# Cross-attention with layer norm: scores from two 64-row halves of the TensorE array

## The chip, the cores and the metric

One core of one Trainium2 chip. The metric is the device time of one execution in microseconds. Five engines work side by side and meet at semaphores: TensorE (PE in the profile; its weight loads, PEld, are listed apart), VectorE (DVE), ScalarE (ACT), GpSimd (POOL) and SyncE (SP), which issues the DMA transfers.

## The reference

Batch 4, 2048 queries and 77 context rows each, width 512, 16 heads of 32. Everything is float32.

```python
qs  = (q @ wq).reshape(Bq, Lq, H, HD).transpose(0, 2, 1, 3)
ks_ = (k @ wk).reshape(Bq, Lk, H, HD).transpose(0, 2, 1, 3)
vs  = (v @ wv).reshape(Bq, Lk, H, HD).transpose(0, 2, 1, 3)
scores = einsum('bhqd,bhkd->bhqk', qs, ks_) / sqrt(HD)
scores = where(mask[:, None, :, :], -inf, scores)
attn_w = softmax(scores, axis=-1)
attn = einsum('bhqk,bhkd->bhqd', attn_w, vs)
out = attn.transpose(0, 2, 1, 3).reshape(Bq, Lq, H * HD) @ wo + q
out = (out - mean) / sqrt(var + EPS) * gamma + beta
```

q is x; k and v are both the context.

## The kernel before

The 8192 query rows are 64 tiles of 128. Everything of a tile is done in two halves of eight heads. To keep float32 accuracy with float32r matmuls, each operand is kept as a high part and a low part (qh and ql, kh and kl, and so on), and each product is three matmuls: high by high, high by low, low by high.

TensorE's order is written out in the loop over t behind L336. For a tile it is: scores of half 0; the output projection of an earlier tile (project_o, 12 matmuls of 512 columns); the transposes of the previous tile's probabilities, half 0 (transpose_p, five of 128 x 128); scores of half 1; the query projection for the tile four ahead (project_q, 12 matmuls of 512 columns); the transposes of half 1. Once in four tiles (t in FIRST, 4, 8, ...) weigh_v follows the scores of half 1, and once (t in SECOND, 5, 9, ...) it follows the scores of half 0. weigh_v multiplies the transposed probabilities of four tiles by the values, in pieces of the array of 64 rows by 32 columns (L315): the keys 0 to 63 from vm, the last 13 from vr.

**Scores.** The heads of a tile come in four groups of four. Partition 32 j + d of qh[:, g] is dimension d of head j of group g, 128 rows in all. kh[:, g, b] is block-diagonal, 4 x 77 = 308 columns: head j's keys stand in rows 32 j to 32 j + 31 and in columns 77 j to 77 j + 76, the rest is zero (memsets L485 and L612; the blocks are filled by L429 and L491). So three matmuls of 308 columns with the query as weights give a bank of scores for 128 queries and four heads, and a half tile is two banks, six matmuls, one after the other (L283). p_s counts one up after each bank.

**Their reader.** VectorE waits for a bank's p_s, adds the mask and writes to pr (L520), twice, then takes the negated maximum of the eight heads (L526). ACT exponentiates head by head (L406, eight instructions), VectorE sums (L533) and inverts (L535), POOL scales into pn (L632, L634), TensorE transposes pn (L293, L295), and ACT copies the result to ptr (L375), which weigh_v reads. VectorE and ACT carry out their instructions in written order, the work for the norm and for the query splits among them. A score block may overwrite a bank once VectorE has read it (v_st).

Of the kernel before, what the change touches and what calls it, by code (L numbers as in the profile page):

```python
# [5 lines left out]
P = 128  # L6
NB, LQ, D, H, HD, LK = 4, 2048, 512, 16, 32, 77
# [3 lines left out]
TB = LQ // P  # L11
GW = 4 * LK
NG = 4
# [23 lines left out]
def outputs(t):  # L37
    return OUTPUTS.get(t, ())


def cross_attention_layernorm(nc, x, xT, ctxT, mask, wq, wk, wv, wo, gamma, beta, out):
    f32, f32r, u8 = mybir.dt.float32, mybir.dt.float32r, mybir.dt.uint8
    ALU = mybir.AluOpType
# [10 lines left out]
    with ctx:  # L54
        def sb(name, shape, dt=f32):
            return ctx.enter_context(nc.sbuf_tensor(name, shape, dt))

        def sem(name):
            return ctx.enter_context(nc.semaphore(name))
# [2 lines left out]
        wql = sb("wql", [P, KT, D], f32r)  # L62
        woh = sb("woh", [P, KT, D], f32r)
        wol = sb("wol", [P, KT, D], f32r)
        kh = sb("kh", [P, NG, NB, GW], f32r)
        kl = sb("kl", [P, NG, NB, GW], f32r)
        vm = sb("vm", [P, NB, 2, 4, HD])
        vr = sb("vr", [P, NB, 2, 4, HD])
        msk = sb("msk", [P, 2, TB, LK], u8)
# [24 lines left out]
        with ExitStack() as start:  # L94
            def early(name, shape):
# [16 lines left out]
        SB, PTB, AVB, MB = bank[0:2], bank[2:4], bank[4:6], bank[6:8]  # L112
# [10 lines left out]
        p_k, p_v, p_q, p_s, p_tp, p_pv, p_o = (  # L123
            sem(n) for n in ("p_k", "p_v", "p_q", "p_s", "p_tp", "p_pv", "p_o"))
# [4 lines left out]
        v_z, v_w, v_k, v_pf, v_ps, v_ql, v_st, v_max, v_sum, v_rec, v_al, v_res, v_bs, v_bn, v_y = (  # L129
            sem(n) for n in ("v_z", "v_w", "v_k", "v_pf", "v_ps", "v_ql", "v_st", "v_max", "v_sum", "v_rec",  # L130
                             "v_al", "v_res", "v_bs", "v_bn", "v_y"))
# [104 lines left out]
        def _(pe):  # L236
            for k in range(KT):
                pe.wait_ge(d_k[k], 32)
                for g in range(NG):
                    mm = nc.tensor.matmul(bank[g][:, 0:NB * LK], wk_sb[:, k, g * P:(g + 1) * P], ctx_sb[:, k, :],  # L240
                                          start=(k == 0), stop=(k == KT - 1))
# [3 lines left out]
            def project_v(b):  # L245
                if b == 0:
                    pe.wait_ge(d_wv, 16)
                if b >= 2:
                    pe.wait_ge(a_v, b - 1)
                for k in range(KT):  # L250
                    last = nc.tensor.matmul(AVB[b % 2][0:LK, :], ctx_sb[:, k, b * LK:(b + 1) * LK], wv_sb[:, k, :],
                                            start=(k == 0), stop=(k == KT - 1))
                last.then_inc(p_v, 1)
# [15 lines left out]
                        n += 1  # L269
                last.then_inc(p_q, 1)  # L270

            def scores(t, groups):
                blk, r = t // 4, t % 4
                for g in groups:
                    i = NG * t + g
                    if t == 0:
                        pe.wait_ge(v_k, 4 * g + 4)
                    pe.wait_ge(v_ql, 4 * blk + g + 1)
                    if i >= 2:
                        pe.wait_ge(v_st, i - 1)  # L280
                    o = SB[i % 2][:, 0:GW]
                    for n, (w, s) in enumerate(((qh, kh), (qh, kl), (ql, kh))):
                        last = nc.tensor.matmul(o, w[blk % 2][:, g, r * P:(r + 1) * P], s[:, g, t // TB, :],  # L283
                                                start=(n == 0), stop=(n == 2))
                    last.then_inc(p_s, 1)

            def transpose_p(t, half):
                n = 2 * t + half
                pe.wait_ge(g_norm, n + 1)
                if n >= 1:  # L290
                    pe.wait_ge(a_pt, n)
                for s in range(4):
                    last = nc.tensor.transpose(PTB[0][:, s * P:(s + 1) * P], pn[:, half, s, :], ident[:])  # L293
                last.then_inc(p_tp, 1)
                nc.tensor.transpose(PTB[1][:, 0:P], pn[:, half, 4, :], ident[:]).then_inc(p_tp, 1)  # L295

            def weigh_v(e):
                t, n, half = STEPS[e]
                b, cols = t // TB, columns(e)
                if e == 0:  # L300
                    pe.wait_ge(d_vm[0], 160)
                    pe.wait_ge(d_vm[1], 160)
                pe.wait_ge(a_pt, 2 * (t + n - 1) + half + 1)
                if e == 0:
                    pe.wait_ge(a_v, NB)
                elif e < E - 1:
                    pe.wait_ge(v_al, 2 * e)
                else:
                    pe.wait_ge(v_st, NG * T)
                for v, first in ((vm, True), (vr, False)):  # L310
                    for j in range(4):
                        for gi in range(2):
                            rows = slice(KM * gi, KM * gi + KM)
                            c = j if first else 4
                            mm = nc.tensor.matmul(av_bank(e, gi)[HD * j:HD * (j + 1), 0:n * P], v[rows, b, half, j, :],  # L315
                                                  ptr[rows, half, c, cols], start=first, stop=not first)
                            if not first and j == 3:
                                mm.then_inc(p_pv, 1)

            def project_o(t):  # L320
                r = t % 4
                misc_free(pe, ("o", t))
                o = misc_bank(("o", t))
                n = 0
                for k in range(KT):
                    pe.wait_ge(v_al, 2 * STEP_OF[t, k // 2] + k % 2 + 1)
                    for w, s in ((ah, woh), (ah, wol), (al, woh)):
                        last = nc.tensor.matmul(o[:], w[:, k, r * P:(r + 1) * P], s[:, k, :],  # L328
                                                start=(n == 0), stop=(n == 3 * KT - 1))
                        n += 1  # L330
                last.then_inc(p_o, 1)
# [1 line left out]
            for i in range(4):  # L333
                project_q(i)
            for t in range(T):
                scores(t, (0, 1))  # L336
                if t == 0:
                    project_v(0)
                if t == 1:
                    pe.wait_ge(g_id, 2)  # L340
                if t in SECOND:
                    weigh_v(SECOND[t])
                elif outputs(t):
                    project_o(outputs(t)[0])
                if t >= 1:
                    transpose_p(t - 1, 0)
                scores(t, (2, 3))
                if t < 3:
                    project_v(t + 1)
                if t in SECOND:  # L350
                    if t == 5:
                        pe.wait_ge(a_w, KT + 1)
                        pe.wait_ge(v_w, KT + 1)
                    project_o(outputs(t)[0])
                for o in outputs(t)[1:]:
                    project_o(o)
                if t in FIRST:
                    weigh_v(FIRST[t])
                    transpose_p(t - 1, 1)
                if t + 4 < T:  # L360
                    project_q(t + 4)
                if t >= 1 and t not in FIRST:
                    transpose_p(t - 1, 1)
# [9 lines left out]
        def _(act):  # L373
# [51 lines left out]
            def keep_k(g):  # L425
                act.wait_ge(p_k, g + 1)
                for j in range(4):
                    rows = slice(32 * j, 32 * j + 32)
                    nc.scalar.activation(kh[rows, g, :, j * LK:(j + 1) * LK],  # L429
                                         bank[g][rows, 0:NB * LK].rearrange("p (b k) -> p b k", b=NB), ACT.Copy,  # L430
                                         scale=SCALE).then_inc(a_k, 1)

# [4 lines left out]
            for k in range(KT):  # L437
                act.wait_ge(d_wq[k], 16)
                keep(wqh[:, k, :], wq_raw[:, k, :]).then_inc(a_w, 1)
                keep_x(k)  # L440
            act.wait_ge(v_z, 1)
            keep_k(0)
            keep_k(1)
            keep_q(0)
            keep_k(2)
            keep_q(1)
            keep_k(3)
# [36 lines left out]
        def _(dve):  # L484
            nc.vector.memset(kh[:].bitcast(f32), 0.0).then_inc(v_z, 1)  # L485

            def low_k(g):
                for j in range(4):
                    rows = slice(32 * j, 32 * j + 32)
                    dve.wait_ge(a_k, 4 * g + j + 1)  # L490
                    nc.vector.scalar_tensor_tensor(  # L491
                        out=kl[rows, g, :, j * LK:(j + 1) * LK],
                        in0=bank[g][rows, 0:NB * LK].rearrange("p (b k) -> p b k", b=NB), scalar=SCALE,
                        in1=kh[rows, g, :, j * LK:(j + 1) * LK].bitcast(f32), op0=ALU.mult,
                        op1=ALU.subtract).then_inc(v_k, 1)

            def mask_all(b):
# [69 lines left out]
            for k in range(KT):  # L567
                dve.wait_ge(a_w, k + 1)
                nc.vector.tensor_tensor(wql[:, k, :], wq_raw[:, k, :], wqh[:, k, :].bitcast(f32),
                                        ALU.subtract).then_inc(v_w, 1)  # L570
            dve.wait_ge(g_z, 1)
            low_k(0)
            low_k(1)
            low_q(0)
            low_k(2)
            low_q(1)
            low_k(3)
# [128 lines left out]
```

## Time and profile before

| | |
|---|---|
| median of three runs | 698.63 us (698.15, 702.37, 698.63) |
| the profiled execution | 700.0 us, span 698.0 us |
| busy, share of the span | PE 92%, PEld 71%, DVE 76%, ACT 73%, POOL 70% |
| granted clock of TensorE over the span | 0.972 |

Busy time is the time in which at least one instruction of the engine is under way. A matmul's duration includes the time its result takes through the array, so matmuls that follow each other overlap in it: the distance between two starts tells what one takes of the engine. In a timeline a row holds one instruction, or a run of like ones with their count. In square brackets stands the idle time before a row and what ended it. Only PEld rows tell when weights begin to load.

### The profile page before, as it was taken

The numbers are of one execution on the slowest core, as the hardware profiler recorded it, in microseconds if no ns is written. First come the engines' busy times: TensorE is split into PE (matmuls) and PEld (weight loads), VectorE is DVE, ScalarE is ACT, GpSimd is POOL, SyncE is SP. The second block draws the span as 40 slices with busy tenths as digits, with TensorE's granted clock in tenths as the row PEclk, the third lists the DMA queues.
The fourth block names the chain that finished last, engine by engine and source line by source line (L and its number), as shares of the span: only waits on it lengthen the run. The fifth ranks groups of instructions, "written<-read, shape, count | busy, mean of one in ns | idle before, by whom it ended". The sixth has DMA issues, their size and how long they took to land. (4 is left out here: it accounts for less than half of the span.)

```text
span 698.0 us, 13011 instructions
## 1 busy us (share of the span) xinstructions
PE 640.0 (92%) x4096; PEld 497.2 (71%) x4096; DVE 529.6 (76%) x1006; ACT 511.5 (73%) x1562; POOL 490.3 (70%) x641
## 2 busy tenths in 40 slices
PE   7989799999999999999999999999999999987454
PEld 4657487777868686877778686868777786865333
DVE  5667587878888878877889878788779888785444
ACT  4667688778877887887787788878788787774340
POOL 6234457897877777788977787777888786775551
PEclk9989999999999999999999999999999999999776
DMA  8532112222231222212222222222222211112112
GB/s 274 190 96 43 32 61 71 83 91 76 92 101 63 88 78 92 89 64 91 91 87 91 65 88 77 92 92 69 83 92 77 77 61 46 62 46 61 61 45 76
DMA packets 36563, 57.78 MB, mean 83 GB/s; under 512 B 8592, under 2 KB 9616, under 8 KB 36496
## 3 DMA queue, kind: packets, MB, share of 16 engines
q1 hardware_dynamic: 36496, 56.96, 24.7%
q8 instruction: 34, 0.56, 0.3%
q14 instruction: 33, 0.27, 0.1%
HBM read 39.53 MB, written 16.78 MB: 81 GB/s over the span
## 5 line engine op out<-in xcount | busy, mean ns | idle before, releaser
L406 ACT ACTIVATE pr<-pr,nm 128x77 f32<-128x77 f32 x1024 | 269.9, 351 | 53.1 <-DVE nm L526 52.9
L632 POOL TENSOR_TENSOR pn<-pr,rec 128x512 f32<-128x512 f32 x128 | 134.9, 1054 | 100.8 <-DVE rec L535 96.3
L520 DVE SCALAR_TENSOR_TENSOR pr<-msk,bank 128x308 f32<-128x308 uint8 x256 | 109.5, 469 | 66.2 <-PE bank L283 66.2
L328 PE MATMUL bank<-woh,ah 128*128 128x512 f32 x256 | 103.1, 403 | 15.3 <-DVE al L542 15.3
L533 DVE TENSOR_REDUCE sm<-pr 128x8 f32<-128x616 f32 x128 | 99.8, 780 | 19.1 <-ACT pr L406 18.9
L267 PE MATMUL bank<-xh,wqh 128*128 128x512 f32 x256 | 103.9, 406 | 2.2 <-DVE ql L508 1.3
L526 DVE TENSOR_REDUCE nm<-pr 128x8 f32<-128x616 f32 x128 | 101.8, 795 | 4.4
L328 PE MATMUL bank<-woh,al 128*128 128x512 f32 x256 | 102.4, 400 | 0.0
L328 PE MATMUL bank<-wol,ah 128*128 128x512 f32 x256 | 102.2, 399 | 0.0
L267 PE MATMUL bank<-xh,wql 128*128 128x512 f32 x256 | 101.0, 394 | 0.0
L267 PE MATMUL bank<-xl,wqh 128*128 128x512 f32 x256 | 100.2, 391 | 0.0
L375 ACT ACTIVATE ptr<-bank 128x512 f32<-128x512 f32 (+1 forms) x256 | 95.5, 426 | 4.8 <-PE bank L293 4.8
L624 POOL TENSOR_TENSOR xl<-xraw,xh 128x512 fp32r<-128x512 f32 x64 | 83.5, 1307 | 20.4 <-ACT xh L375 20.3
L293 PEld LDWEIGHTS bank<-ident,pn 128*128 128x128 f32 x512 | 61.8, 142 | 46.7 <-issue 32.4
L283 PE MATMUL bank<-kh,qh 128*128 128x308 f32 x256 | 88.0, 344 | 2.8 <-DVE pr L520 1.9
L293 PE MATMUL bank<-ident,pn 128*128 128x128 f32 x512 | 80.1, 280 | 5.8 <-POOL pn L634 3.0
L660 POOL TENSOR_TENSOR y<-y,bet 128x512 f32<-128x512 f32 x60 | 77.2, 1287 | 4.7
L283 PE MATMUL bank<-kh,ql 128*128 128x308 f32 x256 | 78.3, 306 | 0.0
L283 PE MATMUL bank<-kl,qh 128*128 128x308 f32 x256 | 78.3, 306 | 0.0
L658 POOL TENSOR_TENSOR y<-y,gam 128x512 f32<-128x512 f32 x60 | 77.3, 1289 | 0.0
L422 ACT ACTIVATE y<-z,rs 128x512 f32<-128x512 f32 x60 | 49.1, 818 | 29.4 <-DMA out<-y 17.1
L542 DVE TENSOR_TENSOR al<-bank,ah 128x512 fp32r<-128x512 f32 (+1 forms) x68 | 41.6, 655 | 37.8 <-ACT ah L375 37.8
(55 smaller groups left out, 1081.2 us busy)
## 6 DMA issues: line engine op xcount, KB each, us to landing
xraw<-xT SPq DMA_DIRECT2D x64, 256.0 KB, 3.0
xres<-x SPq DMA_DIRECT2D x64, 256.0 KB, 2.7
out<-y SPq DMA_DIRECT2D x64, 256.0 KB, 2.0
wk_sb<-wk SPq DMA_DIRECT2D x4, 256.0 KB, 4.1
wq_raw<-wq SPq DMA_DIRECT2D x4, 256.0 KB, 5.8
wv_sb<-wv SPq DMA_DIRECT2D x1, 1024.0 KB, 5.5
wo_raw<-wo SPq DMA_DIRECT2D x1, 1024.0 KB, 6.2
ctx_sb<-ctxT SPq DMA_DIRECT2D x4, 154.0 KB, 3.3
```

Source lines behind the costliest of these rows:

```text
L267: last = nc.tensor.matmul(o[:], w[:, k, m * P:(m + 1) * P], s[:, blk % 2, k, :], start=(n == 0), stop=(n == 3 * KT - 1))
L283: last = nc.tensor.matmul(o, w[blk % 2][:, g, r * P:(r + 1) * P], s[:, g, t // TB, :], start=(n == 0), stop=(n == 2))
L293: last = nc.tensor.transpose(PTB[0][:, s * P:(s + 1) * P], pn[:, half, s, :], ident[:])
L328: last = nc.tensor.matmul(o[:], w[:, k, r * P:(r + 1) * P], s[:, k, :], start=(n == 0), stop=(n == 3 * KT - 1))
L375: return nc.scalar.activation(dst, src, ACT.Copy)
L406: last = nc.scalar.activation(s, s, ACT.Exp, bias=nm[:, t % 2, h:h + 1], scale=1.0)
L520: nc.vector.scalar_tensor_tensor(out=pr[:, 4 * g:4 * g + 4, :], in0=msk[:, b % 2, t % TB, :].unsqueeze(1).broadcast_to([P, 4, LK]), scalar ...
L526: nc.vector.tensor_reduce(nm[:, t % 2, HH * half:HH * half + HH], pr[:, HH * half:HH * half + HH, :], AX.X, ALU.max, negate=True).then_inc ...
L533: nc.vector.tensor_reduce(sm[:, t % 2, hs], pr[:, hs, :], AX.X, ALU.add).then_inc(v_sum, 1)
L624: nc.gpsimd.tensor_tensor(xl[:, n // KT % 2, n % KT, :], xraw[:, n % NX, :], xh[:, n // KT % 2, n % KT, :].bitcast(f32), ALU.subtract).the ...
L632: nc.gpsimd.tensor_tensor(pn[:, half, 0:4, :].rearrange("p s (e k) -> p (s e) k", e=2), pr[:, hs, 0:KM], rec[:, t % 2, hs].unsqueeze(2).br ...
L658: nc.gpsimd.tensor_tensor(y[:, w], y[:, w], gam[:], ALU.mult).then_inc(g_ap, 1)
```

## The change

The heads of a tile are grouped differently. The columns of wq and wk are put in another order before the launch, so that rows 0 to 63 of group g hold two heads and rows 64 to 127 two others, and the scores of the two lie in two banks. kh and kl are then only 154 columns wide: the block of head j stands in columns 77 (j mod 2) onwards. For each group and each of the three products there are two matmuls, one on rows 0 to 63 into SB[0], one on rows 64 to 127 into SB[1], each of 154 columns. The second group of a half tile writes the columns 154 to 307 of the same two banks. What a bank holds at the end (four heads of 77 in the old order), who reads it and every instruction of the other engines are as before; the lines behind L283 have moved by six. p_s counts up at the last two matmuls of the block.

```diff
-        kh = sb("kh", [P, NG, NB, GW], f32r)
-        kl = sb("kl", [P, NG, NB, GW], f32r)
+        kh = sb("kh", [P, NG, NB, 2 * LK], f32r)
+        kl = sb("kl", [P, NG, NB, 2 * LK], f32r)
...
-            def scores(t, groups):
+            def scores(t, half):
+
                 blk, r = t // 4, t % 4
+                groups = (2 * half, 2 * half + 1)
                 for g in groups:
-                    i = NG * t + g
                     if t == 0:
                         pe.wait_ge(v_k, 4 * g + 4)
                     pe.wait_ge(v_ql, 4 * blk + g + 1)
-                    if i >= 2:
-                        pe.wait_ge(v_st, i - 1)
-                    o = SB[i % 2][:, 0:GW]
+                for gi, g in enumerate(groups):
                     for n, (w, s) in enumerate(((qh, kh), (qh, kl), (ql, kh))):
-                        last = nc.tensor.matmul(o, w[blk % 2][:, g, r * P:(r + 1) * P], s[:, g, t // TB, :],
-                                                start=(n == 0), stop=(n == 2))
-                    last.then_inc(p_s, 1)
+                        for rh in range(2):
+                            i = NG * t + 2 * half + rh
+                            if n == 0 and gi == 0 and i >= 2:
+                                pe.wait_ge(v_st, i - 1)
+                            rows = slice(64 * rh, 64 * rh + 64)
+                            mm = nc.tensor.matmul(SB[rh][:, 2 * LK * gi:2 * LK * (gi + 1)],
+                                                  w[blk % 2][rows, g, r * P:(r + 1) * P], s[rows, g, t // TB, :],
+                                                  start=(n == 0), stop=(n == 2))
+                            if n == 2 and gi == 1:
+                                mm.then_inc(p_s, 1)
...
-                    nc.scalar.activation(kh[rows, g, :, j * LK:(j + 1) * LK],
+                    nc.scalar.activation(kh[rows, g, :, j % 2 * LK:(j % 2 + 1) * LK],
...
-                        out=kl[rows, g, :, j * LK:(j + 1) * LK],
+                        out=kl[rows, g, :, j % 2 * LK:(j % 2 + 1) * LK],
...
-        "wq": c(L0_xattn_wq), "wk": c(L0_xattn_wk), "wv": c(L0_xattn_wv), "wo": ...
+        "wq": c(np.asarray(L0_xattn_wq).reshape(D, 2, 2, 2, 2, HD).transpose(0, 1, 3, 2, 4, 5).reshape(D, D)),
+        "wk": c(np.asarray(L0_xattn_wk).reshape(D, 2, 2, 2, 2, HD).transpose(0, 1, 3, 2, 4, 5).reshape(D, D)),
```

TensorE's order around a score block that stands between transposes and an output projection, before (kh, kl, qh, ql are the halves of keys and queries, the number at a row's end its columns; x2 stands for two alike):

```order
L295 MATMUL bank<-ident,pn 128x128
L283 MATMUL bank<-kh,qh 128x308 [waits v_st,v_ql]
L283 MATMUL bank<-kl,qh 128x308
L283 MATMUL bank<-kh,ql 128x308
L283 MATMUL bank<-kh,qh 128x308 [waits v_st,v_ql]
L283 MATMUL bank<-kl,qh 128x308
L283 MATMUL bank<-kh,ql 128x308
L328 MATMUL bank<-woh,ah 128x512 [waits v_al,v_res]
```

and the same place of the changed kernel:

```order
L301 MATMUL bank<-ident,pn 128x128
L287 MATMUL bank<-kh,qh 128x154 [waits v_st,v_ql]
L287 MATMUL bank<-kh,qh 128x154 [waits v_st]
L287 MATMUL bank<-kl,qh 128x154 x2
L287 MATMUL bank<-kh,ql 128x154 x2
L287 MATMUL bank<-kh,qh 128x154 x2
L287 MATMUL bank<-kl,qh 128x154 x2
L287 MATMUL bank<-kh,ql 128x154 x2
L334 MATMUL bank<-woh,ah 128x512 [waits v_al,v_res]
```

The block stays where it was, between the same neighbours. Its waits for VectorE's reading of both banks and for both groups' queries now stand at its first two matmuls. VectorE's own order has not moved; here are its rows for a half tile in the changed kernel:

```order
L526 SCALAR_TENSOR_TENSOR pr<-msk,bank 128x308 [waits p_s,g_norm]
L526 SCALAR_TENSOR_TENSOR pr<-msk,bank 128x308 [waits p_s]
L532 TENSOR_REDUCE nm<-pr 128x8 [waits v_st]
L539 TENSOR_REDUCE sm<-pr 128x8 [waits a_exp]
L541 RECIPROCAL rec<-sm 128x8 [waits v_sum]
```

They are those of before, with the line numbers moved by six.

## Rows read from the trace of the kernel before

**Rows 1.** Part 1 of the page: busy us (share of the span) x instructions.

```profile
PE 640.0 (92%) x4096; PEld 497.2 (71%) x4096; DVE 529.6 (76%) x1006; ACT 511.5 (73%) x1562; POOL 490.3 (70%) x641
```

**Rows 2.** Windows: stretch, its us, PE busy us (x instructions), granted clock, DMA share, GB/s.

```profile
40.00:80.00 40.00, 33.21 (x167) 0.87 0.21 49
100.00:600.00 500.00, 487.15 (x3219) 1.00 0.24 81
640.00:698.00 58.00, 27.61 (x213) 0.76 0.16 55
```

**Rows 3.** Timeline of PE (start us, us, instruction, xcount): projection, scores, weigh_v.

```profile
311.33 0.40 PE L267 MATMUL bank<-xl,wqh 128*128 128x512 f32 x1
...
313.63 0.40 PE L267 MATMUL bank<-xh,wql 128*128 128x512 f32 x1
313.86 0.31 PE L283 MATMUL bank<-kh,qh 128*128 128x308 f32 x1
...
314.58 0.30 PE L283 MATMUL bank<-kh,ql 128*128 128x308 f32 x1
314.81 0.66 PE L315 MATMUL bank<-ptr,vm 64*32 64x512 f32 x8
```

**Rows 4.** Waits: engine and line, whom it waited for: us, times, longest us.

```profile
PE bank L315 <- ACT ptr L375: 18.5, 16, 4.4
```

**Rows 5.** Timeline of PE: the end of the scores before the other weigh_v.

```profile
307.45 0.30 PE L283 MATMUL bank<-kh,ql 128*128 128x308 f32 x1
308.61 1.09 PE L315 MATMUL bank<-ptr,vm 64*32 64x512 f32 x16 [0.85 <-ACT ptr L375]
```

**Rows 6.** Timeline of ACT before that weigh_v.

```profile
305.81 2.11 ACT L406 ACTIVATE pr<-pr,nm 128x77 f32<-128x77 f32 x8 [0.22 <-DVE nm L526]
307.82 0.73 ACT L375 ACTIVATE ptr<-bank 128x512 f32<-128x512 f32 x2
```

**Rows 7.** Timeline of DVE before that weigh_v.

```profile
299.09 0.86 DVE L520 SCALAR_TENSOR_TENSOR pr<-msk,bank 128x308 f32<-128x308 uint8 x2 [1.07 <-PE bank L283]
...
304.09 0.85 DVE L520 SCALAR_TENSOR_TENSOR pr<-msk,bank 128x308 f32<-128x308 uint8 x2
...
305.69 0.68 DVE L508 TENSOR_TENSOR ql<-bank,qh 128x512 fp32r<-128x512 f32 x1
```

**Rows 8.** Groups by line and shape: busy us, mean ns | idle before.

```profile
L283 PE MATMUL bank<-kh,qh 128*128 128x308 f32 x256 | 88.0, 344 | 2.8 <-DVE pr L520 1.9 <-DVE ql L508 0.9
```

**Rows 9.** Timeline of PEld (weight loads): weigh_v, and the transposes behind it.

```profile
308.61 0.18 PEld L315 LDWEIGHTS bank<-ptr,vm 64*32 64x32 f32 x16 [1.11 <-ACT ptr L375]
309.06 0.16 PEld L315 LDWEIGHTS bank<-ptr,vr 64*32 64x32 f32 x8 [0.27 <-issue]
309.49 0.16 PEld L315 LDWEIGHTS bank<-ptr,vr 64*32 64x32 f32 x8 [0.27 <-issue]
310.49 0.42 PEld L293 LDWEIGHTS bank<-ident,pn 128*128 128x128 f32 x4 [0.84 <-issue]
```

**Rows 10.** Timeline of PE near the start: value projection, 512 columns, unsplit array.

```profile
27.71 3.59 PE L251 MATMUL bank<-wv_sb,ctx_sb 128*77 128x512 f32 x8
```

**Rows 11.** Timeline of PEld: two float32r loads after a pause.

```profile
222.23 0.19 PEld L267 LDWEIGHTS bank<-xh,wqh 128*128 128x128 f32 x1 [0.69 <-DVE ql L508]
222.34 0.19 PEld L267 LDWEIGHTS bank<-xl,wqh 128*128 128x128 f32 x1
```

**Rows 12.** Timeline of PEld: the last load of the scores, the first of weigh_v.

```profile
314.44 0.19 PEld L283 LDWEIGHTS bank<-kh,ql 128*128 128x128 f32 x1
314.80 0.18 PEld L315 LDWEIGHTS bank<-ptr,vm 64*32 64x32 f32 x16 [0.18 <-issue]
```

**Rows 13.** Timeline of PE: the last eight passes of weigh_v.

```profile
309.92 0.64 PE L315 MATMUL bank<-ptr,vr 64*32 64x512 f32 x8
```

**Rows 14.** Timeline near the start: the memset of kh, the first copies into kh.

```profile
1.82 4.17 DVE L485 MEMSET kh<- 128x4928 f32 x1 [1.82 <-issue]
...
15.94 3.53 ACT L429 ACTIVATE kh<-bank 32x308 fp32r<-32x308 f32 x8
```

More of the change, by code:

```diff
@@ L335, in _ @@
             for t in range(T):
-                scores(t, (0, 1))
+                scores(t, 0)
                 if t == 0:
@@ L346, in _ @@
                     transpose_p(t - 1, 0)
-                scores(t, (2, 3))
+                scores(t, 1)
                 if t < 3:
@@ L491, in low_k @@
                     nc.vector.scalar_tensor_tensor(
-                        out=kl[rows, g, :, j * LK:(j + 1) * LK],
+                        out=kl[rows, g, :, j % 2 * LK:(j % 2 + 1) * LK],
                         in0=bank[g][rows, 0:NB * LK].rearrange("p (b k) -> p b k", b=NB), scalar=SCALE,
-                        in1=kh[rows, g, :, j * LK:(j + 1) * LK].bitcast(f32), op0=ALU.mult,
+                        in1=kh[rows, g, :, j % 2 * LK:(j % 2 + 1) * LK].bitcast(f32), op0=ALU.mult,
                         op1=ALU.subtract).then_inc(v_k, 1)
@@ L697 @@
         "mask": c(np.asarray(mask_BxSxS2_bk1).reshape(T, P, LK).transpose(1, 0, 2).reshape(P, T * LK)),
-        "wq": c(L0_xattn_wq), "wk": c(L0_xattn_wk), "wv": c(L0_xattn_wv), "wo": c(np.asarray(L0_xattn_wo).reshape(2, 4, 2, HD, D).transpose(0, 2, 1, 3, 4).reshape(D, D)),
+        "wq": c(np.asarray(L0_xattn_wq).reshape(D, 2, 2, 2, 2, HD).transpose(0, 1, 3, 2, 4, 5).reshape(D, D)),
+        "wk": c(np.asarray(L0_xattn_wk).reshape(D, 2, 2, 2, 2, HD).transpose(0, 1, 3, 2, 4, 5).reshape(D, D)),
+        "wv": c(L0_xattn_wv), "wo": c(np.asarray(L0_xattn_wo).reshape(2, 4, 2, HD, D).transpose(0, 2, 1, 3, 4).reshape(D, D)),
         "gamma": c(L0_xattn_gamma), "beta": c(L0_xattn_beta),
```

## The prediction, made before the changed kernel had run

> **What bounds the kernel now.** I read the page's busy shares first. PE shows 640.0 us of 698.0, far above VectorE's 529.6 [rows 1], and from 100 to 600 us it is busy for 487 of 500 us at a granted clock of 1.00, TensorE's upper level of 2.4 GHz [rows 2]. Matmul durations contain the pipeline's tail, so I then took start-to-start distances from the timeline. A 512-column projection matmul starts every 0.23 us ((313.63 - 311.33) / 10), a 308-column score matmul every 0.144 us ((314.58 - 313.86) / 5), with no hole between the two kinds [rows 3]. Six score matmuls of one half tile thus hold TensorE for 0.86 us. The pattern repeats every four tiles. In it PE stands still for one thing only: one weigh_v in four tiles waits for ACT's copy of the transposed probabilities [rows 4, 5]. All else is matmuls end to end, so what the change adds to or takes from PE's stream shows in the time one to one, except in the stretch that ends in that wait.
>
> **What sets that wait.** The last score matmul before it ends streaming near 307.45 + 0.14 = 307.59, and weigh_v starts at 308.61 [rows 5]: 1.02 us, of which 0.09 would be there anyway (below), so 0.93 is the wait. ACT's two ptr copies end at 308.55, right behind exponentials that waited for VectorE's maximum [rows 6]. VectorE worked without a recorded pause from 299.09, where it had waited 1.07 us for scores of the tile before, through 304.09 to 305.69 (only the first row has a wait) [rows 7]. The wait hangs on the moment at which a bank of scores is handed to VectorE.
>
> **What is removed.** 768 score matmuls (3 x 256, [rows 8]) of 308 columns. **What is added.** 1536 of 154 columns on 64 rows each. By the slope between the two distances, (0.230 - 0.144) / 204 = 0.42 ns a column, one takes 0.144 - 154 x 0.00042 = 0.08 us. If the two row halves run side by side, six pairs of a half tile stream in 6 x 0.08 = 0.48 us instead of 0.86.
>
> *Do matmuls on different rows run side by side?* weigh_v uses eight 64-row, 32-column pieces of the array. Eight of its passes of 512 columns start within one group, and the next eight start 0.43 us later (309.06, 309.49, [rows 9]). On the unsplit array one such pass alone takes at most 3.59 / 8 = 0.45 us [rows 10]. So eight cost the time of one, and both row halves are among them. I take it as shown.
>
> *Weight loads.* Each of the 24 matmuls brings its own load of 128 weight columns. After a pause, where nothing streams, a float32r load begins at 222.23 and the next at 222.34: the first takes 0.11 us [rows 11]. Today it hides under a 0.144 us matmul; under a 0.08 us one it cannot. Whether a load of 64 rows is cheaper than one of 128 no row shows. Bounds: 0.055 (half the rows, half the time) and 0.11. I take 0.11. The Trainium skill's page "TensorE: Matmul & The Clock Gate", section "LDWEIGHTS (loading the stationary operand)", says that the time goes by columns and not by rows, which speaks against this change; with it the value is also 0.11, without it the sum below would fall to near nothing.
>
> *Loads of both halves at once?* In weigh_v eight loads of 32 columns go out in a bunch and its second round's loads are already under way while the first round streams (a row of x16 from 308.61, lasting 0.18 in all, [rows 9]). One 128-column load every 0.11 us is 0.027 for 32 columns; 16 in a row would need 0.44. So loads of different pieces overlap, and I take a pair of half loads as 0.11. The other bound, one after the other, is 0.22 a pair.
>
> *Switching the shape of the array.* Going from full-array scores into weigh_v, the last score matmul ends streaming at 314.58 + 0.14 = 314.72, and the next load starts only at 314.80; between full-array matmuls the load comes a whole matmul ahead (314.44 for 314.58, [rows 3, 12]). Coming back, the last eight passes start at 309.92, stream 0.43, and the next load starts at 310.49: 0.14, of which 0.05 is the spread of the eight, so 0.09 [rows 9, 13]. A switch costs 0.08 to 0.09 of standstill and lays the first load bare. No row shows a switch between 128 and 64 rows at full width; bounds 0 and this, and I take this, the only switch that the trace has. The Trainium skill's page "TensorEngine Tiling (Array Packing)", section "Key Properties", says that changing the tiling mode drains TensorE; these rows agree, and by that rule every score block now begins and ends with a drain.
>
> **The sum for a half tile.** Standstill 0.08, first load 0.11, five more pairs at 0.11 = 0.55, last stream 0.08: the scores are done at 0.82. Then 0.09 and the bare load of the projection that follows, 0.11: 1.02 against 0.86, that is +0.16 us. Where weigh_v follows, the exit switch is paid today, and the block is 0.82 against 0.86: -0.04. Of the eight half tiles in four tiles, two are followed by weigh_v.
>
> **The wait moves too.** Before, the first bank was ready after three matmuls, 0.43 us into the block; now both complete together, at 0.82. VectorE (two operations, 0.85 us together) starts 0.39 later, and so does all that follows until ptr [rows 6, 7]. PE's own way to that weigh_v grows by 0.16 + 0.16 - 0.04 = 0.28 only. So the stretch, three of the eight half tiles, grows by 0.39 and the wait by 0.11. The other five: 4 x 0.16 - 0.04 = +0.60. Per four tiles +1.0 us, and 15 such groups: +15 us.
>
> **The rest.** The first four tiles and the tail wait for other things: from 40 to 80 us PE is busy 33 of 40, from 640 on 28 of 58 [rows 2]; 0 to 1.3 us (8 x 0.16) each, I take +1. The memset of kh halves, but it ends at 5.99 and ACT's first copy into kh starts at 15.94 [rows 14]: nothing, cover 10 us. The K copies (L429, L491) and their low parts keep count and size; the weights' column order is set before the launch; SP's queue is the same. The second matmul of a block now waits for VectorE's reading of the second bank, 0.4 us earlier than before; VectorE is done at 304.94 and the next block starts at 307.45 - 0.78 = 306.67 [rows 5, 7], cover 1.7 us. The first also waits for the query part of the second head group, ready at 306.37 [rows 7], 0.3 us ahead; VectorE comes 0.39 later and PE 0.32, so 0.2 are left, and a miss would only eat into the ptr wait. If PE did get faster, the next to be late is that ptr copy.
>
> Sum: 700.0 (the profiled execution; its span is 698.0) + 15 + 1 = 716. The runs' median, 698.63, is 1.4 lower, so I forecast 715, 2.3% slower. With the bounds on the switch and the small terms the forecast's own range is 707 to 725.
>
> **Rivals.**
> *A: no standstill between 128 and 64 rows (the other side).* For it: the pieces keep all 128 columns, unlike weigh_v's. Against: both switches that the trace shows cost it. The half block is then 5 x 0.11 + 0.08 and some 0.03 = 0.66, -0.20 each; scores are handed over at 0.63, 0.20 later than now. In the stretch of the wait +0.20, the other five -1.0: -0.8 per four tiles, x 15 = -12 us, 687. It decides once the two switches, bare loads included, cost under 0.20 a block (0.86 - 0.66) instead of 0.36.
> *B: switch as forecast, but half loads take 0.055.* Block 0.08 + 0.06 + 5 x 0.08 + 0.08 = 0.62, with exit 0.82: -0.04. Handed over at 0.62, +0.19; the other five 4 x -0.04 - 0.24 = -0.40; -0.2 x 15 = -3: 696, no change. Against: 32-column loads' bunch says nothing on rows. Both A and B: 6 x 0.08, about -0.4 a block, handed over +0.08; -1.9 x 15 = -29: 670.
> *C: half loads run one after the other.* The block grows by six further 0.11 = 0.66 to 1.68, +0.82 (+0.62 before weigh_v). The stretch of the wait: 2.26 less the 0.93 swallowed = 1.33; the rest 3.90; 5.2 x 15 = 78: 778. Against: the overlap of weigh_v's loads.
> *D: in part,* pairs of loads at 0.15: +0.40 and +0.20 a block, handed over +0.63; 0.63 + 1.80 = 2.4 x 15 = 37: 736.
>
> **Chances.** Forecast 0.48, A 0.14, B 0.10, A and B together 0.04, C 0.12, D 0.10, something else 0.02. Measurement tells 1% from no change. Faster by over 1% (under 691.6): A, the pair and a rest, 0.19. Within 1%: B, 0.11. Slower: 0.70. The range 686 to 745 takes in A, B, the forecast and D, and leaves out the pair and C, 0.16 with the ends of the others some 0.2.
>
> **What would show it.** In the changed kernel's timeline: pairs of score matmuls starting together, pairs every 0.11 us (0.08 refutes the load price, 0.22 the overlap); a load that starts 0.08 after the last transpose has streamed, and one 0.09 after the last score (a load issued ahead there refutes the switch); VectorE's first score operation right at the block's end; the wait for ptr near 1.0 us, still there. The forecast is wrong if the period of four tiles does not grow by 1.0 us.

## The result, and the profile after

The changed kernel takes 716.12 us (median of four runs, 714.52 to 717.58), the kernel before 700.5 us in the runs beside them: a ratio of 1.0217, with a 95% interval of 1.0157 to 1.0277. It is 2.2% slower; 715 were forecast. The profiled execution has a span of 715.6 us, 17.6 more than that of before.

The same line of the page as in [rows 1], and the windows of [rows 2]:

```profile
PE 657.1 (92%) x4864; PEld 487.5 (68%) x4864; DVE 527.1 (74%) x1006; ACT 511.5 (71%) x1562; POOL 487.5 (68%) x641
```

```profile
40.00:80.00 40.00, 32.42 (x203) 0.86 0.21 49
100.00:600.00 500.00, 486.55 (x3741) 1.00 0.23 79
640.00:698.00 58.00, 36.85 (x296) 0.78 0.14 49
```

TensorE is again the only engine near the span. From 100 to 600 us it is busy as long as before; it only gets less done. Busy time does not show the standstills at a switch either: they are shorter than the tail of the matmul before them, which counts as busy.

The score block between transposes and a projection, first PE's timeline (start us, duration us; x2 are two matmuls, here those of both row halves), then PEld's:

```profile
305.83 0.38 PE L299 MATMUL bank<-ident,pn 128*128 128x128 f32 x2
306.05 0.27 PE L301 MATMUL bank<-ident,pn 128*128 128x128 f32 x1
306.25 0.34 PE L287 MATMUL bank<-kh,qh 64*128 64x154 f32 x2
306.42 0.28 PE L287 MATMUL bank<-kl,qh 64*128 64x154 f32 x2
...
306.87 0.27 PE L287 MATMUL bank<-kh,ql 64*128 64x154 f32 x2
307.07 0.50 PE L267 MATMUL bank<-xh,wqh 128*128 128x512 f32 x1
307.41 0.40 PE L267 MATMUL bank<-xl,wqh 128*128 128x512 f32 x1
```

```profile
306.25 0.19 PEld L287 LDWEIGHTS bank<-kh,qh 64*128 64x128 f32 x2 [0.17 <-issue]
306.36 0.19 PEld L287 LDWEIGHTS bank<-kl,qh 64*128 64x128 f32 x2
...
306.80 0.19 PEld L287 LDWEIGHTS bank<-kh,ql 64*128 64x128 f32 x2
307.07 0.19 PEld L267 LDWEIGHTS bank<-xh,wqh 128*128 128x128 f32 x1
307.18 0.19 PEld L267 LDWEIGHTS bank<-xl,wqh 128*128 128x128 f32 x1
```

What to see: a pair lasts 0.27 to 0.28 us, no longer than one matmul does (0.27, in the series kernel below), so both halves start together. Pairs come every 0.11 us ((306.87 - 306.42) / 4), in step with their loads ((306.80 - 306.36) / 4).

A row of PE has to be read with care here. It begins when the matmul before it has streamed, even if its own load is still under way. The first pair's load runs from 306.25 to 306.36, where the next one starts, and the next row of PE begins at 306.42: so 154 columns stream in 0.06 to 0.07 us. (With 76 columns, in the first experiment below, the second row comes 0.13 after the first and not 0.17.)

The way in: the last transpose, begun at 306.05 and followed by nothing, had streamed its 0.11 us ((306.05 - 305.83) / 2) by 306.16, and the scores' first load starts only at 306.25. Between full-array matmuls a load starts a whole matmul early. The way out: the last pair's load runs from 306.80 to 306.91, its stream ends near 306.98, and the projection's load starts at 307.07. Its second matmul starts at 307.41, so its first streamed from 307.41 - 0.23 = 307.18. Both ends are bare, each with a standstill of 0.09 and a load of 0.11.

The sum closes: 0.09 + 6 x 0.11 + 0.07 + 0.09 + 0.11 = 1.02, and from 306.16 to 307.18 are 1.02 us, the forecast's figure; before, a block held 0.86.

The other place that the forecast spoke of, the weigh_v that waits for ptr. PE and its entry of the table of waits in the changed kernel, then two PE rows of the kernel before that [rows 5] need for the comparison:

```profile
316.77 0.66 PE L321 MATMUL bank<-ptr,vm 64*32 64x512 f32 x8 [0.92 <-ACT ptr L381]
...
356.21 0.66 PE L321 MATMUL bank<-ptr,vm 64*32 64x512 f32 x8 [0.93 <-ACT ptr L381]
```

```profile
PE bank L321 <- ACT ptr L381: 18.4, 16, 4.1
```

```profile
298.28 0.27 PE L295 MATMUL bank<-ident,pn 128*128 128x128 f32 x1
...
346.98 0.66 PE L315 MATMUL bank<-ptr,vm 64*32 64x512 f32 x8 [0.86 <-ACT ptr L375]
```

And the changed kernel's VectorE and ACT on the way to it:

```profile
307.25 0.86 DVE L526 SCALAR_TENSOR_TENSOR pr<-msk,bank 128x308 f32<-128x308 uint8 x2 [1.42 <-PE bank L287]
```

```profile
315.98 0.74 ACT L381 ACTIVATE ptr<-bank 128x512 f32<-128x512 f32 x2
```

Before, VectorE began 0.81 us after the last transpose of the block (298.28 to 299.09, [rows 7]), now 1.20 (306.05 to 307.25): 0.39 later, as forecast. From there to weigh_v it is 9.52 us in both (299.09 to 308.61, [rows 5]; 307.25 to 316.77). The wait itself grew by 0.07 (0.85 [rows 5] to 0.92), where 0.11 were forecast. All 16 such waits together are still 18.4 us against 18.5 [rows 4], since the longest, near the end, is 0.3 shorter. From one such weigh_v to the next it was 346.98 - 308.61 = 38.37 us, now 356.21 - 316.77 = 39.44: +1.07 for four tiles where +1.0 was forecast.

Not every group of four tiles is like this one. Once in 16 tiles the query projection also waits for VectorE's ql, in both kernels. The kernel before, then the changed one:

```profile
192.63 0.66 PE L315 MATMUL bank<-ptr,vm 64*32 64x512 f32 x8 [0.85 <-ACT ptr L375]
...
222.23 0.50 PE L267 MATMUL bank<-xh,wqh 128*128 128x512 f32 x1 [0.44 <-DVE ql L508]
...
231.86 0.66 PE L315 MATMUL bank<-ptr,vm 64*32 64x512 f32 x8 [1.02 <-ACT ptr L375]
```

```profile
197.93 0.66 PE L321 MATMUL bank<-ptr,vm 64*32 64x512 f32 x8 [0.93 <-ACT ptr L381]
...
237.88 0.66 PE L321 MATMUL bank<-ptr,vm 64*32 64x512 f32 x8 [0.88 <-ACT ptr L381]
```

These four tiles took 39.23 us and now take 39.95: +0.72 only, and the wait for ptr shrinks there. Over the whole run, the first waiting weigh_v comes 1.1 us later than before (75.93 and 77.02), the 14 distances from it to the fifteenth add up to 14.9 more (ten of +1.07, three of +0.72, the first of +2.0), and what follows it is 1.6 longer: 17.6 in all.

### The profile page after: what moved, and what is told of

It reads as the page before. It is cut to its first block and busy times, and to the rows that moved or that the text cites. A ratio compares the mean times of both kernels' runs of the same rounds, so it can differ in the third digit from the quotient of the medians.

```text
span 715.6 us, 14421 instructions
## 1 busy us (share of the span) xinstructions
PE 657.1 (92%) x4864; PEld 487.5 (68%) x4864; DVE 527.1 (74%) x1006; ACT 511.5 (71%) x1562; POOL 487.5 (68%) x641
## 5 line engine op out<-in xcount | busy, mean ns | idle before, releaser
L334 PE MATMUL bank<-woh,ah 128*128 128x512 f32 x256 | 109.6, 428 | 15.0 <-DVE al L548 15.0
L267 PE MATMUL bank<-xh,wqh 128*128 128x512 f32 x256 | 106.9, 417 | 2.5 <-DVE ql L514 1.5
L287 PE MATMUL bank<-kh,qh 64*128 64x154 f32 x512 | 81.6, 306 | 2.9 <-DVE pr L526 1.4
L287 PE MATMUL bank<-kl,qh 64*128 64x154 f32 x512 | 72.9, 275 | 0.0
L287 PE MATMUL bank<-kh,ql 64*128 64x154 f32 x512 | 72.3, 274 | 0.0
L287 PEld LDWEIGHTS bank<-kh,qh 64*128 64x128 f32 x512 | 50.8, 187 | 29.4 <-issue 27.1
```

The source lines that it names most:

```text
L267: last = nc.tensor.matmul(o[:], w[:, k, m * P:(m + 1) * P], s[:, blk % 2, k, :], start=(n == 0), stop=(n == 3 * KT - 1))
L287: mm = nc.tensor.matmul(SB[rh][:, 2 * LK * gi:2 * LK * (gi + 1)], w[blk % 2][rows, g, r * P:(r + 1) * P], s[rows, g, t // TB, :], start=(n ...
```

## The experiments

Each ran beside the kernel before; the ratio is to that. "Period" is the time from one waiting weigh_v to the next, four tiles, in an ordinary group.

| kernel | median us | ratio (95%) | period us |
|---|---|---|---|
| before | 699.5 to 700.9 | 1 | 38.37 |
| changed | 716.12 | 1.0217 (1.0157 to 1.0277) | 39.44 |
| 76 columns | 713.34 | 1.0183 (1.0157 to 1.0208) | 39.2 |
| 308 columns on 64 rows | 733.58 | 1.047 (1.043 to 1.0509) | 40.7 |
| 154 columns on 128 rows | 746.73 | 1.066 (1.0636 to 1.0685) | 41.6 |
| before, banks alternating | 704.60 | 1.0073 (1.0043 to 1.0104) | 38.6 |
| changed, halves in series (two runs) | 736.12 | 1.0511 (1.044 to 1.0581) | 40.9 |
| changed, halves in threes | 718.06 | 1.0244 (1.0191 to 1.0297) | 39.5 |
| before, 3 matmuls moved | 689.55 | 0.9857 (0.9806 to 0.9909) | 37.7 |
| before, 6 matmuls moved | 686.64 | 0.9806 (0.9764 to 0.9848) | 37.6 |
| changed, 6 matmuls moved | 709.72 | 1.0134 (1.0089 to 1.0178) | 38.9 |

### Is the pairs' distance the load's?

```diff
-  SB[rh][:, 2 * LK * gi:2 * LK * (gi + 1)] ... s[rows, g, t // TB, :]
+  SB[rh][:, 2 * LK * gi:2 * LK * gi + LK - 1] ... s[rows, g, t // TB, 0:LK - 1]
```

> The changed kernel with 76 moving columns a score matmul instead of 154 (every second head's scores are left out); loads, waits and switches stay. My theory (pairs keep the distance of one weight load, 0.11 us): only the last stream of a block is shorter, 0.03 us, so 4 tiles take 0.2 us less than in the changed kernel, 3 us in all: 712 to 716, pairs still every 0.11 us. Rival (the pairs' distance is streaming plus something fixed for a matmul): pairs at 0.05 to 0.08 us, a block 0.2 to 0.3 shorter, 690 to 703.

PE's timeline of this kernel:

```profile
308.30 0.30 PE L287 MATMUL bank<-kh,qh 64*128 64x76 f32 x2
308.43 0.28 PE L287 MATMUL bank<-kl,qh 64*128 64x76 f32 x2
...
308.88 0.28 PE L287 MATMUL bank<-kh,ql 64*128 64x76 f32 x2
```

With half the columns the pairs still come every 0.11 us ((308.88 - 308.43) / 4), and the time falls by 3 us only. A score matmul in this block does not cost its columns. The rival is out. It costs the load of its 128 weight columns: float32r loads also start 0.11 apart where the matmuls do not press them (307.07 and 307.18 above, with the matmuls 0.34 apart).

### Loads alone, without a switch

```diff
-  rows = slice(64 * rh, 64 * rh + 64)
+  rows = slice(0, P)
```

> The changed kernel with all 128 rows in each of the 24 score matmuls of 154 columns (its scores are not those of the reference): no change of shape of the array, but 24 loads that follow each other. My theory: the distance is that of a load, 0.11, though the stream takes 0.08: block 12 x 0.11 = 1.3 us, no standstill, handed over 0.87 later; per four tiles 0.87 + 5 x 0.46 = 3.2 us, 745 to 755. Rival (loads hide; the distance is the stream's 0.08): block 0.96, 704 to 708.

```profile
310.40 0.43 PE L287 MATMUL bank<-kh,qh 128*128 128x154 f32 x2
310.67 0.39 PE L287 MATMUL bank<-kl,qh 128*128 128x154 f32 x2
...
311.56 0.39 PE L287 MATMUL bank<-kh,ql 128*128 128x154 f32 x2
```

Here a row x2 holds two matmuls one after the other, and they take 0.22 us ((311.56 - 310.67) / 4), 0.11 a matmul. The same 24 loads a tile, now all over the same 128 rows, do not overlap: 12 steps a block instead of six. No bare end is seen: the block begins 0.03 us after the start of the last transpose (310.37 and 310.40), as in the kernel before. Its first matmuls wait for the same semaphores as those of the changed kernel, so it is not these waits that lay the ends bare there. The load's price, which was taken from one place after a pause [rows 11], holds within the stream. Pairs of 64-row loads also take 0.11. Two loads of 0.055 one after the other would do the same; the series kernel below rules that out, where loads on one half alone come every 0.11. So a load costs the same on 64 rows as on 128, the lower bound of 0.055 falls, and rival B with it. The Trainium skill's rule that a load's time does not depend on its rows ("TensorE: Matmul & The Clock Gate", "LDWEIGHTS (loading the stationary operand)") holds here.

### The switch alone

```diff
-        kh = sb("kh", [P, NG, NB, 2 * LK], f32r)
-        kl = sb("kl", [P, NG, NB, 2 * LK], f32r)
+        kh = sb("kh", [P, NG, NB, GW], f32r)
+        kl = sb("kl", [P, NG, NB, GW], f32r)
...
-                            mm = nc.tensor.matmul(SB[rh][:, 2 * LK * gi:2 * LK * (gi + 1)],
+                            mm = nc.tensor.matmul(SB[rh][:, 0:GW],
```

The blocks of the heads stand at columns 77 j again.

> The changed kernel with kh and kl kept 308 columns wide and score matmuls of 308 columns on 64 rows (the scores of the first group of a half tile are overwritten). This is the switch of shape alone: loads hide again under streams. My theory (halves side by side, pairs every 0.144; two standstills of 0.09 and two bare loads of 0.11 a block): block 1.26 instead of 0.86 us before, handed over 0.63 later, +2.4 us per four tiles, 736 to 742. Rival 1 (two halves with long streams share a port and run one after the other): pairs 0.29, over 790. Rival 2 (no standstill, the excess was all loads): 700.

```profile
307.49 0.27 PE L301 MATMUL bank<-ident,pn 128*128 128x128 f32 x1
307.69 0.41 PE L287 MATMUL bank<-kh,qh 64*128 64x308 f32 x2
307.94 0.30 PE L287 MATMUL bank<-kl,qh 64*128 64x308 f32 x2
...
308.50 0.30 PE L287 MATMUL bank<-kh,ql 64*128 64x308 f32 x2
308.73 0.50 PE L334 MATMUL bank<-woh,ah 128*128 128x512 f32 x1
```

Pairs of 308 columns every 0.14 us ((308.50 - 307.94) / 4): streams on both halves lie side by side at full length, and loads hide again. So one block streams for just as long as in the kernel before, and all its excess, 34 us in the run, is the two ends of each block and the later handing over. Rivals 1 and 2 are out, and with 2 the forecast's rival A: a tile of the array that keeps all 128 columns is not spared the switch. The drain that the Trainium skill's page on array packing states for a change of mode ("TensorEngine Tiling (Array Packing)", "Key Properties") is what these rows show, 0.09 us each time: from 307.49 + 0.11 = 307.60 to the first pair at 307.69, whose load still has to run, and from 308.50 + 0.14 = 308.64 to the projection's at 308.73. The expectation was 2 us too high (736 to 742 against 733.58), its period was right (+2.4 expected, 40.73 - 38.37 = 2.36); the groups with the wait for ql grew by 1.6 only.

### The handing over alone

The kernel before, its six matmuls a half tile in another order:

```diff
-  for g in groups:
-      for n, (w, s) in enumerate(((qh, kh), (qh, kl), (ql, kh))):
+  for n, (w, s) in enumerate(((qh, kh), (qh, kl), (ql, kh))):
+      for g in groups:
```

> The kernel before, but the six score matmuls of a half tile alternate between the two banks (high by high for both groups, then high by low, then low by high), so the first bank is handed to VectorE after five matmuls instead of three: 0.28 us later. TensorE's work is the same. My theory (the wait before every second weigh_v hangs on that handing over): the wait grows by 0.28 in four tiles, 15 times, 4 us: ratio 1.006, the distance from one such weigh_v to the next 38.65 instead of 38.37. Rival (other slack takes it up): no change, 38.37.

The two waiting weigh_v of one period:

```profile
274.11 1.09 PE L316 MATMUL bank<-ptr,vm 64*32 64x512 f32 x16 [1.14 <-ACT ptr L376]
...
312.71 1.09 PE L316 MATMUL bank<-ptr,vm 64*32 64x512 f32 x16 [1.14 <-ACT ptr L376]
```

The wait shown is 1.14 us where it was 0.85 [rows 5], the period 38.60, and the time 0.7% up, its interval clear of 1. TensorE's work is unchanged, and alternating between the banks costs it nothing: from the last transpose to the projection are still 0.96 us, as before (306.27 to 307.23; before, 324.11 to 325.07). So in the kernel before, the moment at which the first bank is handed over sets the time, in the one stretch of three half tiles that ends in the ptr wait.

### Do halves overlap, and from how far?

```diff
-  for gi, g in enumerate(groups):
-      for n, (w, s) in enumerate(...):
-          for rh in range(2):
+  for rh in range(2):
+      for gi, g in enumerate(groups):
+          for n, (w, s) in enumerate(...):
```

> The changed kernel with the twelve score matmuls of a half tile in another order: the six on rows 0 to 63 first, then the six on rows 64 to 127. Same matmuls, loads and switches, but neighbours now use the same rows. My theory (loads of the same rows follow each other at 0.11 us, only loads of different rows overlap): the block is 1.6 instead of 1.03 us, the wait before every second weigh_v disappears, +4.5 us per four tiles over the kernel before, 765 to 775. Rival (rows do not matter, loads overlap anyway): 716.

It came to 736.12: my number was too high by 29 us or more, the rival's too low by 20. PE's timeline of a block, then part of PEld's:

```profile
310.08 0.34 PE L287 MATMUL bank<-kh,qh 64*128 64x154 f32 x1
310.25 0.27 PE L287 MATMUL bank<-kl,qh 64*128 64x154 f32 x1
310.37 0.27 PE L287 MATMUL bank<-kh,ql 64*128 64x154 f32 x1
310.37 0.38 PE L287 MATMUL bank<-kh,qh 64*128 64x154 f32 x2
...
311.00 0.27 PE L287 MATMUL bank<-kh,ql 64*128 64x154 f32 x1
```

```profile
310.19 0.19 PEld L287 LDWEIGHTS bank<-kl,qh 64*128 64x128 f32 x1
310.29 0.19 PEld L287 LDWEIGHTS bank<-kh,ql 64*128 64x128 f32 x1
310.37 0.22 PEld L287 LDWEIGHTS bank<-kh,qh 64*128 64x128 f32 x2
```

Up to 310.37 only the first half is at work, and its loads start 0.11 apart (310.08, 310.19, 310.29): one load on 64 rows takes 0.11 by itself. At 310.37 two matmuls start together: the third on the first half's rows and the seventh in program order, the first on the other half's rows. The seventh is known by its record in the trace, which carries the wait for VectorE's reading of the second bank that only this matmul has. It and its load went past the fourth, fifth and sixth, which were waiting for their loads. From then on both halves run side by side, the second 0.30 us behind (310.08 and 310.37), and the last start comes 0.92 after the first (311.00 - 310.08) where the changed kernel has 0.62. So loads of the same rows follow each other, and TensorE looks ahead, but not past all six. The next kernel was made to test that:

```diff
-          for n, (w, s) in enumerate(...):
-              for rh in range(2):
+          for rh in range(2):
+              for n, (w, s) in enumerate(...):
```

> The changed kernel with the row half changing after every three matmuls instead of after every one (and not after six, as in the series kernel, where the second half's first matmul started just after the third had started, past three that were waiting). Theory: TensorE looks past up to three matmuls that wait for their rows and starts one on free rows, so with threes nothing is lost: pairs overlap all through, block about 0.83 and 716 as in the changed kernel, up to 719. Rival (only neighbours overlap, and the series kernel's overlap had another cause): the block is nine or more steps of 0.11, over 730.

```profile
313.02 0.35 PE L287 MATMUL bank<-kh,qh 64*128 64x154 f32 x2
...
313.64 0.28 PE L287 MATMUL bank<-kh,ql 64*128 64x154 f32 x2
```

The first and the last row of a block: 0.62 us, as in the changed kernel (306.25 to 306.87), and 718.06 us. Looking past three costs nothing. That it is three and not more in every case is worked out from one pattern and not shown.

### The wait filled

Six of the 12 matmuls (or three) of the query projection moved ahead of the weigh_v that waits (KF is 2 or 1; project_q itself changes only so that it can be made in two parts):

```diff
   if t in FIRST:
+      if t + 4 < T:
+          project_q(t + 4, range(0, KF))
       weigh_v(FIRST[t])
       transpose_p(t - 1, 1)
   if t + 4 < T:
-      project_q(t + 4)
+      project_q(t + 4, range(KF, KT) if t in FIRST else range(KT))
```

> The kernel before, with the first three matmuls (0.69 us) of the query projection moved ahead of the weigh_v that waits for ptr. Theory: TensorE's 0.93 us of waiting in four tiles is not needed by anyone; 0.69 of it is filled: 37.7 instead of 38.4 us per four tiles, 10 us less, 689. Rival (ACT, which waits for this weigh_v before its next exponentials, gives it back later): 697 to 700.

> The same with six matmuls (1.39 us) ahead. Theory: all 0.93 us are filled and weigh_v comes 0.46 later than before: 37.4 us per four tiles, 14 us less, 685. Rival (ACT and VectorE, held up by the later weigh_v, make another wait): no better than with three, 689, or worse.

The one with six:

```profile
302.76 0.40 PE L269 MATMUL bank<-xh,wql 128*128 128x512 f32 x1
303.09 1.09 PE L318 MATMUL bank<-ptr,vm 64*32 64x512 f32 x16
...
310.28 0.27 PE L298 MATMUL bank<-ident,pn 128*128 128x128 f32 x1
310.43 0.38 PE L286 MATMUL bank<-kh,qh 128*128 128x308 f32 x1
```

weigh_v starts 0.33 us after the last of the moved matmuls, which is its 0.23 of streaming and the switch; no wait is left there. 14 us less were expected, 13.1 measured (699.72 to 686.64). It beats both kernels by a clear interval: 1.9% under the kernel before. Three matmuls more bring only 3 us over the first three, as the remaining 0.24 us of wait in four tiles would have it. The period fell by 0.80 (38.37 to 37.57), not by the 0.93 filled: the score block behind the second weigh_v now starts 0.15 after the transpose's start (310.28 to 310.43) instead of 0.03, which gives 0.12 back.

> The changed kernel with six matmuls of the query projection ahead of the same weigh_v. Theory: its wait (1.0 us in four tiles) is filled as well: 38.45 us per four tiles, 702, and the change then costs TensorE's own time alone, 6 x 0.16 - 2 x 0.04 = 0.9 to 1.0 us in four tiles against the kernel before with the same filling, 15 us. Rival (the later handing over costs elsewhere once this wait is filled): over 20 us between the two.

Here the theory fell and the rival held: 709.72, 23.1 us above the same filling of the kernel before (3.4%). Two things were left out. Moving the projection between scores and weigh_v gives that score block an exit of its own, so seven of eight blocks pay, not six (two were to gain 0.04). And the block behind the second weigh_v of four tiles now waits inside. PE, then VectorE:

```profile
324.75 0.60 PE L290 MATMUL bank<-kh,qh 64*128 64x154 f32 x2
325.02 0.44 PE L290 MATMUL bank<-kl,qh 64*128 64x154 f32 x2
...
325.84 0.50 PE L337 MATMUL bank<-woh,ah 128*128 128x512 f32 x1
```

```profile
324.11 0.85 DVE L531 SCALAR_TENSOR_TENSOR pr<-msk,bank 128x308 f32<-128x308 uint8 x2
```

The block ran from 324.75 to the projection at 325.84, 1.09 us where 0.82 are usual (306.25 to 307.07). Its first row holds two matmuls that did not start together: in the trace the one on rows 0 to 63 starts at 324.75, the one on rows 64 to 127 at 325.01, 0.05 after VectorE has read the second bank (324.11 + 0.85 = 324.96). Where before the second bank was needed three matmuls later, both must now be free for the first pair. The same block of the filled kernel before is 0.12 longer than usual, as said, so this one accounts for 0.27 - 0.12 = 0.15 of the difference. Seven blocks at 0.17, this 0.15 and -0.02 at the block before the second weigh_v make 1.32; the periods' difference is 38.93 - 37.57 = 1.36. That VectorE's reading is what the half waits for is read from the times and the order of waits; it was not tried alone.

## Why the prediction was right

The likeliest case came, and by its own steps.

- *TensorE's stream is the bound.* Shown from both sides: filling 0.93 us of waiting in four tiles took 0.80 off the period and 1.9% off the time, and what was added per block came out in the time.
- *Row halves run side by side.* A pair lasts as long as one matmul; with 308 columns pairs still come every 0.14, as single ones do over 128 rows.
- *A load costs 0.11 on 64 rows.* 0.11 with 154 columns and with 76, 0.11 on one half alone, and 0.11 on 128 rows. The stream, 0.08 forecast and 0.06 to 0.07 measured, shows only behind the last pair.
- *Loads of the two halves overlap.* Five distances from the first start of a block to the last with alternating halves (0.62 us), 0.92 us in series, eleven distances on the same rows.
- *Two ends of 0.20 each.* Measured 0.20 and 0.20; block 1.02 against 1.02. Rival A falls to the kernel with 308 columns, where nothing but the ends and the handing over is added and 34 us appear.
- *Handed over 0.39 later, +0.39 in three half tiles, +1.0 in four tiles.* Measured 0.39 for the first and 1.07 for the last in an ordinary group, so PE's own way grew a little more than forecast and the wait a little less (0.07 and not 0.11). The handing over alone did what it should in the kernel before.
- *Fifteen groups at 1.0, +15; start and tail +1.* Measured +14.9 over fourteen groups and 2.7 outside them.

One reading of the prediction was wrong: that PE stands still for one thing only in the four tiles. Once in 16 tiles it also waits 0.44 us for VectorE's ql, and such a group grew by 0.72 and not by 1.07. That the fourteen groups still make 14.9 is luck in part, since the first of them grew by 2.0; why that one did was not looked into. The other miss is small: a block grew by nearer 0.17 than 0.16.

That 715 stands so near 716 has luck in it too. The forecast added 16 to a base of 698.63; the spans differ by 17.6, but the medians by 15.6 only, from 700.5 to 716.12.

Where the change could have gained, from 0.86 to 0.48 us of streaming a block, it did: the streams are that short. But the block is six loads long, 0.66, and the last stream, the two standstills and the projection's bare load add 0.36. Each alone would have left the block near or under 0.86, by estimates from these figures that no run tried: hidden ends give about 0.73 (0.66 + 0.07), hidden loads between bare ends 0.82 (6 x 0.07 + 0.40) to 0.88 (with 0.08 a stream). Both together give 1.02.

## What to carry to other kernels

Splitting the array by rows halves the columns streamed, not the weight loads: below the length of a load (here 0.11 us; by an estimate from 0.144 us at 308 columns and the slope of 0.42 ns, what some 230 moving columns take) a shorter stream brings nothing. Count what each entry to and exit from another shape of the array lays bare, and set it against one block's saving; here a block of six pairs was too short for it. And look for the one place where the bounding engine waits: six independent matmuls moved there brought 1.9%, about what this change costs.

## What the runs showed of the hardware that was not expected

With the halves in series, a matmul on rows 64 to 127 started before three that stood ahead of it in the program and waited for rows 0 to 63 (310.37, above): TensorE started matmuls on different rows out of program order, loads included. For this kernel it means that strict alternation is not needed; changing halves after three matmuls costs the same (718.06 and 716.12, whose ranges overlap), after six it costs 0.30 us a block.
